# Perceiver layer on one core: context transposes issued one by one behind long matmuls, with two PSUM banks, full-width transposes of the maxima and one projection triple a step

## The reference

```python
x = x + cross_attention(layernorm(x), ctx, ctx, Wq, Wk, Wv, Wo)   # 32 query heads, 8 key/value heads of 16
x = x + self_attention(layernorm(x), Wq, Wk, Wv, Wo)              # rotary, causal, the same head counts
x = x + (layernorm(x) @ dequantised_3bit(w).T + bias)             # 512 x 512
```

## Time and profile before

| | |
|---|---|
| Time, median of 3 runs (lowest to highest) | 391.9 us (389.97 to 392.42) |
| The profiled execution's own time | 393.17 us |
| Its span, first to last instruction | 391.4 us |
| Mean granted clock of TensorE | 0.974 |
| Busy: PE, PEld, DVE, ACT, POOL | 352.6, 242.6, 241.3, 200.6, 99.8 us |

### The profile page before, as it was taken

The page is one execution under the profiler, slowest core; times in us unless marked ns, Lnnn a source line. Parts: engine busy times, 40 slices in busy tenths (PEclk is TensorE's granted clock), DMA queues, the critical chain, the costliest instruction groups (busy, mean ns, idle before and its releaser), DMA issues.

```text
span 391.4 us, 8460 instructions
## 1 busy us (share of the span) xinstructions
PE 352.6 (90%) x2937; PEld 242.6 (62%) x2940; DVE 241.3 (62%) x439; ACT 200.6 (51%) x356; POOL 99.8 (26%) x190
## 2 busy tenths in 40 slices
PE   0889859999999999999999999994789898989996
PEld 0654545667667676767767676663346665876565
DVE  2568746756656666576566666565466336796753
ACT  3454332865655755765666656555375532336410
POOL 0030811331330421421313313313001213371411
PEclk9999979999999999999999999998599899999999
DMA  7926059746858649659559469999600000000002
GB/s 262 291 45 146 1 100 178 178 81 164 176 78 167 143 97 177 105 118 193 80 127 203 69 143 193 163 141 198 71 2 3 0 2 1 2 2 0 2 27 80
DMA packets 37542, 41.16 MB, mean 105 GB/s; under 512 B 17632, under 2 KB 32224, under 8 KB 35424
## 3 DMA queue, kind: packets, MB, share of 16 engines
q1 hardware_dynamic: 37304, 40.51, 51.8%
q10 hardware_dynamic: 216, 0.36, 0.5%
HBM read 24.07 MB, written 1.05 MB: 64 GB/s over the span
## 4 chain that ended last, share of the span: by engine, by line
PE 70%; DVE 12%; DMA 7%; ACT 3%; SPq 3%; issue 2%; POOL 2%; ACTq 0%; POOLq 0%; DVEq 0%
PE b_t L888 8%; PE b_d L923 7%; PE b_s L935 7%; PE b_c L948 7%; PE b_v L898 5%; PE b_k L898 4%; PE b_k L900 3%; PE b_k L899 3%; PE b_v L899 3%; PE b_v L900 3%; DMA qstack<-region 3%; DMA cx<-in_ctx_dram 2%; DMA region<-in_L_attn_Wo_dram 2%; PE b_c L1012 2%; SPq L334 2%
## 5 line engine op out<-in xcount | busy, mean ns | idle before, releaser
L682 DVE TENSOR_REDUCE negmax<-b_s 128x1 f32<-128x512 f32 x128 | 88.1, 689 | 83.1 <-PE b_s L935 77.1
L549 ACT ACTIVATE region<-b_c 128x512 f32<-128x512 f32 x128 | 76.8, 602 | 66.3 <-PE b_c L948 65.8
L935 PE MATMUL b_s<-kstack,qstack 96*128 96x512 bf16 x128 | 51.1, 399 | 6.4 <-DMA qstack<-region 3.4
L539 ACT ACTIVATE cT_h<-b_t 128x512 fp32r<-128x512 f32 x64 | 38.2, 597 | 35.3 <-PE b_t L888 34.6
L888 PE MATMUL b_t<-ident_sb,cx 128*128 128x128 f32 x256 | 42.0, 288 | 11.9 <-DMA cx<-in_ctx_dram 10.0
L948 PE MATMUL b_c<-qstack,kstack 108*128 108x128 bf16 x512 | 50.2, 221 | 1.8 <-ACT qstack L520 1.8
L948 PEld LDWEIGHTS b_c<-qstack,kstack 108*128 108x128 bf16 x512 | 38.7, 99 | 20.3 <-issue 5.0
L432 POOL TENSOR_TENSOR mparts<-negmax,zeros 128x4 bf16<-128x4 f32 x32 | 6.4, 199 | 166.4 <-DVE negmax L682 166.4
L700 DVE TENSOR_TENSOR cT_l<-b_t,cT_h 128x512 fp32r<-128x512 f32 x64 | 43.6, 682 | 5.8 <-ACT cT_h L539 5.8
L888 PEld LDWEIGHTS b_t<-ident_sb,cx 128*128 128x128 f32 x256 | 29.9, 145 | 20.1 <-issue 14.9
L935 PEld LDWEIGHTS b_s<-kstack,qstack 96*128 96x128 bf16 x128 | 12.6, 98 | 42.1 <-issue 26.1
(11 more groups left out here) (368 smaller groups left out, 589.0 us busy)
## 6 DMA issues: line engine op xcount, KB each, us to landing
cx<-in_ctx_dram SPq DMA_DIRECT2D x16, 1024.0 KB, 6.9
kstack<-kparts SPq DMA_DIRECT2D x96, 128.0 KB, 4.6
qstack<-region SPq DMA_DIRECT2D x96, 32.0 KB, 5.5
xs<-in_x_dram SPq DMA_DIRECT2D x1, 1024.0 KB, 10.3
region<-in_L_xattn_Wq_dram SPq DMA_DIRECT2D x1, 1024.0 KB, 12.8
cx<-in_L_xattn_Wo_dram SPq DMA_DIRECT2D x8, 128.0 KB, 7.6
cx<-in_L_attn_Wq_dram SPq DMA_DIRECT2D x1, 1024.0 KB, 8.1
region<-in_L_attn_Wo_dram SPq DMA_DIRECT2D x8, 128.0 KB, 5.7
```

The lines of the kernel that those rows point to most:

```text
L539: nc.scalar.activation(cT_h[:, c], b_t[:], ACT.Copy).then_inc(ctx_high, 1)
L549: nc.scalar.activation(pT[:, g], b_c[g % 2][:].rearrange("p (a n) -> p a n", a=KT), ACT.Exp, scale=SCALE).then_inc(exp_ready, 1)
L682: nc.vector.tensor_reduce(negmax[:, n % 2, g:g + 1], b_s[:], AX, ALU.max, negate=True).then_inc(max_ready, 1)
L935: nc.tensor.matmul(b_s[:], qstack[0:STACK, n % 4, g], kstack[0:STACK, n % 4, g], start=True, stop=True).then_inc(s_ready, 1)
```

## The change

- Context transposes go out one by one. `ctx_ahead` puts one piece behind the score product and one behind the projection triple of each step, so that a chunk of four takes two steps (an even g and the next one); pieces of chunk 0 of the next batch take g = 6 and 7. Chunks take turns in two banks, `b_t` and `b_x`, and a chunk waits for the low part of the chunk before the last.
- There is one triple a step in a fixed order. The values' chunks 2 and 3 of a batch fall to g = 0 and 1 of the next slot.
- The maxima are transposed from `mwide`, 128 columns wide, zero outside the twelve, into `b_d`. A wait for `mrows_ready` guards that place.
- The value transposes write `b_v`. The copy `vT` moves from g = 1 to g = 2 on ScalarE, behind `cT_h`. The values' copy on VectorE moves to g = 3, the raw output's transposes and the normalisation to g = 4, the normalised output's transpose to g = 6.
- The copy `oT` moves from VectorE (g = 6) to ScalarE (g = 7, between the exponential and the broadcast of the maxima), and at g = 2 and 3 the broadcast and `o_raw` move one step later.
- SyncE issues the next context load ahead of a slot's key parts, and drops a wait for `st_ready` before these.
- `residual1` no longer waits for `tail_weights_loaded`; `residual2` does.

```diff
@@ banks
-        b_y = (b_t, b_s)
+        b_y = (b_x, b_s)
+        b_tx = (b_t, b_x)
+        o_rows = b_d[:, 2 * P:4 * P]
+        o_cols = b_d[:, 2 * P:3 * P]
+        m_rows = b_d[:, 3 * P:3 * P + P // 2].bitcast(BF16)
@@ sync, slot
+                if live(n + 3, trip) and (looped(trip) or n >= -1):
+                    sp.wait_ge(ctx_transposed, transposed)
+                    load_ctx(n + 3, trip)
                 if live(m, trip):
-                    if looped(trip) or n >= 1:
-                        sp.wait_ge(st_ready, through)
...
                     for part, done in enumerate((k_high, k_mid, k_low)):
                         sp.wait_ge(done, split)
                         stack_keys(m, part)
-                        if part == 1 and live(n + 3, trip):
-                            sp.wait_ge(ctx_transposed, transposed)
-                            load_ctx(n + 3, trip)
@@ scalar, slot
+                    if g == 7 and live(n - 2, trip):
+
+                        m = n - 2
+                        wait(act, o_transposed, 1, m, 1, trip)
+                        tile = m // BPT + trip
+                        nc.scalar.activation(oT[:, tile, :, S * (m % BPT):S * (m % BPT) + S],
+                                             o_cols.rearrange("p (r t) -> p r t", r=R), ACT.Copy).then_inc(oT_ready, 1)
                     if g == 7 and live(n, trip):
                         max_rows(n, 0, trip)
@@ tensor
+            def ctx_part(m, c, a, trip):
+
+                if a == 0:
+                    if c == 0:
+                        wait_ring(pe, ctx_loaded, m, trip)
+                    wait(pe, ctx_low, C, m, c - 1, trip)
+                    if not looped(trip) and (m, c) == (1, 1):
+                        pe.wait_ge(xhT_ready, 1)
+                piece = nc.tensor.transpose(b_tx[c % 2][:, P * a:P * a + P], cx[:, m % 2, a, P * c:P * c + P], ident[:])
+                if a == KT - 1:
+                    piece.then_inc(ctx_transposed, 1)
+
+            def ctx_ahead(n, g, second, trip):
+
+                m, c = (n + 2, g // 2 + 1) if g < 6 else (n + 3, 0)
+                if live(m, trip):
+                    ctx_part(m, c, 2 * (g % 2) + second, trip)
...
-                nc.tensor.transpose(b_x[STACK:ROWS, 0:P // 2].bitcast(BF16),
-                                    mparts[:, half].rearrange("p k j -> p (k j)"), ident_h[:]).then_inc(m_transposed, 1)
+                wait(pe, mrows_ready, 2, m, half, trip)
+                nc.tensor.transpose(m_rows, mwide[:, half], ident_h[:]).then_inc(m_transposed, 1)
...
+                    if g < 2 and live(n + 1, trip):
+                        project(n + 1, 1, 2 + g, trip)
+                    if g >= 2 and live(n + 2, trip) and n != -1:
+                        project(n + 2, *((0, 0), (0, 1), (1, 0), (0, 2), (1, 1), (0, 3))[g - 2], trip)
+                    ctx_ahead(n, g, 1, trip)
@@ residual1
                     pe.wait_ge(weights_loaded, 16 * G)
-                    pe.wait_ge(tail_weights_loaded, 16 * G)
```

More of the change, by code:

```diff
@@ L251, in perceiver, with slots @@
         FIRST, LAST, TRIPS = -2, B + 1, 3
-        def slots(eng, slot, start, after=None):
+        def slots(eng, slot, start, after=None, trips=TRIPS):
             for n in range(FIRST, start):
@@ L257, in slots @@
                     after(n)
-            with eng.Fori(0, TRIPS) as trip:
+            with eng.Fori(0, trips) as trip:
                 for n in range(start, start + 4):
                     slot(n, trip)
-            for n in range(start + 4 * TRIPS, LAST + 1):
+            for n in range(start + 4 * trips, LAST + 1):
                 slot(n, 0)
@@ L533, in slot @@
                         nc.scalar.activation(vT[:], b_v[:], ACT.Copy).then_inc(vT_ready, 1)
[L534 to L542, removed]
+                    if g == 3 and live(n - 1, trip):
                         max_rows(n - 1, 1, trip)
@@ L894, in project @@
                 if c == 0:
-                    wait(pe, vT_ready if which else k_res, 1, m, 0, trip)
+                    wait(pe, v_ready if which else k_res, 1, m, 0, trip)
                 out = (b_k, b_v)[which][:]
@@ L919, in times_v @@
                         pe.wait_ge(pv_zero, 1)
+                else:
+                    wait(pe, oT_ready, 1, m, 0, trip)
                 for a in range(KT):
@@ L936, in slot @@
                                          start=True, stop=True).then_inc(s_ready, 1)
-                    if g == 0 and live(n + 2, trip):
-                        ctx_chunk(n + 2, 0, trip)
+                    if not looped(trip) and (n, g) == (FIRST, 0):
+                        for a in range(KT):
+                            ctx_part(0, 0, a, trip)
+                    ctx_ahead(n, g, 0, trip)
                     if live(n - 1, trip):
@@ L956, in slot @@
                     if g == 2 and live(n - 1, trip):
-                        wait(pe, mrows_ready, 2, n - 1, 1, trip)
                         max_rows(n - 1, 1, trip)
                     if g == 3 and live(n + 1, trip):
-                        m = n + 1
-                        wait(pe, vT_ready, 1, m, 1, trip)
+                        wait(pe, vT_ready, 1, n + 1, 1, trip)
+                        for a in range(KT):
+                            last = nc.tensor.transpose(b_v[:, P * a:P * a + P], vT[:, P * a:P * a + P], ident[:])
@@ L962, in slot @@
+                        last.then_inc(v_transposed, 1)
+                    if g == 4 and live(n - 2, trip):
+                        m = n - 2
+                        wait(pe, oraw_ready, 1, m, 1, trip)
+                        wait(pe, oT_ready, 1, m, 0, trip)
                         if live(n - 1, trip):
                             wait(pe, mrows_ready, 2, n - 1, 2, trip)
-                        for a in range(KT):
-                            last = nc.tensor.transpose(b_x[:, P * a:P * a + P], vT[:, P * a:P * a + P], ident[:])
@@ L966, in slot @@
-                        last.then_inc(v_transposed, 1)
-                    if g == 3 and live(n - 2, trip):
-                        m = n - 2
-                        wait(pe, oraw_ready, 1, m, 1, trip)
                         for half in range(2):
-                            last = nc.tensor.transpose(b_d[:, P * (2 + half):P * (3 + half)], o_raw[:, half], ident[:])
+                            last = nc.tensor.transpose(o_rows[:, P * half:P * half + P], o_raw[:, half], ident[:])
                         last.then_inc(oraw_transposed, 1)
-                    if not looped(trip) and n == -2 and g == 1:
-                        pe.wait_ge(wkv_split, 2)
@@ L1029, in transpose_rows @@
                 pe.wait_ge(xn_ready[norm], t + 1)
-                for semaphore, value in ((vT_ready, B), (max_ready, G * B), (exp_ready, G * B))[t:t + 1] if norm == 0 else ():
+                for semaphore, value in ((v_ready, B), (max_ready, G * B), (exp_ready, G * B))[t:t + 1] if norm == 0 else ():
                     pe.wait_ge(semaphore, value)
@@ L1134, in head @@
                 if (n, g) == (-1, 7):
-                    for which, chunks in ((0, C), (1, C - 1)):
+                    for which, chunks in ((0, C), (1, 2)):
                         for c in range(chunks):
@@ L1149, in _ @@
             pe.wait_ge(ident_loaded, 16)
-            slots(pe, slot, 2)
+            slots(pe, slot, 2, trips=2)
             late(steps)
```

82 lines of the change are left out of this document (33 added, 49 removed).

## The result

The changed kernel takes **387.21 us** (median of 6 runs, 386.0 to 389.67), the kernel before 392.25 us in the same comparison (389.97 to 393.31): 5.0 us less, ratio 0.9885 (95% interval 0.9844 to 0.9926). Forecast were 381.7 us and 374 to 389. The time lies in the range, but less than half of the forecast gain of 10.2 us came. The profiled execution took 386.58 us with a span of 384.8 (before 391.4). That pair differs by 6.6 us, not 5.0: the one run is slower than its median, the other faster.

The account below looks back on a forecast made before the run. TensorE's issue order was taken to bound the loop, and waits the ends. Savings of 2.2 (loop) + 0.6 + 1.4 - 1.0 (start) + 7.0 (end) = 10.2 us against the 391.9 median gave 381.7 us, range 374 to 389.

Parts of the forecast that it names:

- The row prices of the loop: TensorE in the loop: transpose 0.11, full-width maximum 0.06, product behind an L948 group or full-width maximum 0.28 us.
- the unknown y: Loop: cost of a triple's first product behind times_v, between 0.28 and 0.42 us, taken as 0.42.
- rival 2: Loop: a transpose costs 0.06 behind a long matmul, 7.8 us more saved, 374; chance 0.04.
- The edge wait: Slot's edge: TensorE waits 0.53 us for ScalarE's broadcast of the maxima, behind the oT copy, replacing 0.13.
- Rivals 1 and 4: Slot's edge: 1, wait does not come, 375.4, chance 0.12; 4, wait grows to 0.7 or more, 384 to 387, chance 0.10.
- The first of the g = 5 group waits for cT_l: Loop before the change: that context transpose costs 0.31 us instead of 0.11, waiting on the single bank.
- rival 5: In the loop, cT_l comes late for all four chunks, so TensorE stands four times a slot: 401; chance 0.07.
- The end, 7.0: First output projection: the 5.83 us weight wait goes, with 1.0 of slow clock behind it; 7.0 us saved.
- rival 3: At the end, weight wait becomes key-part wait (m = 15), giving 3 not 7, or start loses 2.5: 386; chance 0.17.
- The tail, 0: Stretch from slot n = 15 to the end: no term in the sum, so 0 us of change.
- The start, 1.0 less 2.0: Before the loop: 1.0 us lost by the later vT copy, 1.4 and 0.6 saved in slots n = 0 and 1.
- The earlier context load costs nothing: SP's queue: load issued two steps earlier and read a slot later, so free unless ctx arrives later than 15 us.

Follow-up runs that it names:

- the ctx(3) run: The changed kernel with the context load of batch 3 issued between the query parts of slots 0 and 1, not behind both: 386.86 us.

## Why the prediction was wrong, step by step

- **The row prices of the loop: right.** 0.11, 0.06 and 0.28 came as costed, and the unknown y is 0.43 (taken 0.42). The measured 0.11 in every slot puts rival 2 out. By the sections of the Trainium skill that the prediction names ("TensorE: Matmul & The Clock Gate", "Back-to-back issue gap" and "LDWEIGHTS (loading the stationary operand)") I had worked out 0.06, from the isolated gap; the first of them says itself that this gap is too small for a stream of weight loads and matmuls and gives about 81 ns there. The 0.11 of these fp32 transposes is above both.
- **The edge wait: right** in size (0.53) and cause, shown by the run that takes it away. Rivals 1 and 4 are out. The loop slot is 14.91, forecast 14.96; with slots 2 and 13, shorter still, the loop gave 3.3 for 2.2. A wait of 0.06 for a maximum at g = 5, which also went, was not in my sum.
- **"The first of the g = 5 group waits for cT_l": right.** VectorE's cT_l ends at 167.72, the weight load of the group starts at 167.77, and in all twelve loop slots the first transpose starts 0.06 behind the end of cT_l:

```profile
167.04 0.68 DVE L700 TENSOR_TENSOR cT_l<-b_t,cT_h 128x512 fp32r<-128x512 f32 x1
```

```profile
167.77 0.42 PEld L888 LDWEIGHTS b_t<-ident_sb,cx 128*128 128x128 f32 x4 [0.15 <-DVE cT_l L700]
```

  It is no price of an fp32 transpose behind a short bf16 product: the transposes of vT (L965) stand behind the same kind of group, and the first of them adds 0.12. The saving of 0.20 came. No gap in front of L912 from a late cT_l, the sign of rival 5, stands in the loop of the changed kernel.
- **The end, 7.0: the mechanism right, the size too large.** In the pair of traces slot n = 14 gives 5.5. What is missing is the slow clock, which stays for the first product (1.92) in this trace and not in that of the ctx(3) run, where the slot is another 1.3 shorter. On the kernel before, the moved wait alone gives 4.9, and there slot 15 does wait 1.90 for its key parts, the thing I had named as next and priced at nothing. That is rival 3 in part, but not in the changed kernel, whose key parts land 3 us before they are needed.
- **The tail, 0: the step that failed.** The sum has no term for the stretch from n = 15 to the end. I looked at the move of ScalarE's o_raw to g = 3 only in the loop. In slot n = 17 another table puts a wait for VectorE at g = 2, and o_raw went behind it: TensorE waits 2.54 us, and the whole costs 3.8 us in the medians.
- **The start, 1.0 less 2.0: the gain did not come.** Forecast was 1.0 us won up to slot n = 2; the pair of traces has 0.6 lost. Counted from the first transpose, n = 2 begins after 72.0 to 73.2 us in the five traces of the kernel before and its edits, and after 72.3 to 73.5 in the three traces of the changed kernel whose start is untouched. I counted TensorE's work in slots 0 and 1, but the landing of the key parts of m = 1 bounds where n = 1 can start. Undoing what could be undone gave nothing that can be told.
- **"The earlier context load costs nothing": true in the loop, but for a wrong reason.** I wrote that it is read a slot later. Its first reader had moved to g = 6 of the same slot, and without the earlier issue the change is 16.6 us slower.

Put together: 10.2 forecast, less 1.5 at the end, 3.8 at o_raw and 1.6 at the start, plus 1.1 in the loop, is 4.4; measured are 5.0. The parts are from single traces but for the 3.8, so the agreement to 0.6 us is better than they can vouch for. Only o_raw is shown by a run of its own; the shortfalls at the end and at the start are read from traces, which differ by 1 us and more in these stretches.

## What to carry to other kernels

A step moved by one place in a loop body is also moved in the unrolled first and last passes; look there for what another table has put between the old place and the new. When the transposes or loads of a later batch move ahead, ask for each load who its first reader is now. And before work is taken off the critical engine, look at what waits last at the edge of a pass: 5.9 us of real saving stayed invisible here until three instructions of another engine changed places and one copy in the last slot went back.

## What the runs showed of the hardware that I had not expected

- A stall can cost more than its length. 2.54 us of idle TensorE in the last slot cost 3.8 us in the medians (4.3 in a second pair of kernels), with the granted clock down to 0.83 in one trace and 0.71 in another over the same 10 us. A wait of 1.53 to 1.69 us in slot n = 14 was followed by the slow clock in three traces and not in seven.
- A 12-column stationary operand is dearer than a 128-column one behind a bf16 group: 0.15 against 0.06 for the transpose, 0.43 against 0.28 for the projection product behind it. Behind the 17-column times_v the width made no difference to the transpose itself (0.16 and 0.17), but the product behind it went from 0.43 to 0.28 there too.
- A context load of 1 MB landed 4.7 to 5.1 us after its issue in most loop slots when it was issued ahead of the key parts, and 6.5 to 7.8 us in nearly all when it was issued between them.
